# Gated cross-attention and expert layer: the waits of the first attention batch placed where they are needed, the first mask loaded early

## The chip, the cores and the metric

The kernel runs on one core of a Trainium2 chip. The metric is the device time of one execution in microseconds; the profile times every instruction and every DMA packet of one execution.

## The reference

Two layers work on 8 batches of 224 rows of 512 values. The first is a gated cross-attention: 16 heads of 32 values, 750 context rows, an integer mask. The second routes rows to 8 experts.

```python
Q, K, V = proj(_layernorm(x), W_q), proj(ctx, W_k), proj(ctx, W_v)     # Q, K turned by position
scores = jnp.einsum('bhqd,bhkd->bhqk', Q, K) / jnp.sqrt(jnp.float32(D_K))
scores = jnp.where(mask == 0, jnp.float32(-jnp.inf), scores)
attn = jax.nn.softmax(scores, axis=-1)
x = x + jnp.tanh(g_xattn[0]) * (jnp.einsum('bhqk,bhkd->bhqd', attn, V) ... @ W_o)
logits = jnp.einsum('bsd,ed->bse', _layernorm(x), gate_w)
gating, idx = jax.lax.top_k(softmax(logits).T, k)                      # k = 56 rows of 224 per expert
x = x + jnp.tanh(g_ffn[0]) * scatter(gating * (silu(x_in @ w_gate) * (x_in @ w_up)) @ w_down)
```

## The kernel before, in words

The program has three parts, one after the other; each is a block with one hand-written instruction stream per engine, and all engines meet at a barrier between blocks.

**`project_context`** (about 0 to 289 us of the span) makes K and V of all 8 batches, in four pairs. TensorE multiplies, ScalarE copies V out of PSUM (`v_out`) and makes the high half of K (`k_split`), VectorE rotates K and makes the low half. SyncE (SP), which issues most DMAs, stores both to DRAM (`k_split<-k_split`, `v_rows<-v_out`). The last pair also prepares the queries of batch 0 (`qs`). At its end GpSimd (POOL) waits for its own stores of `qs`, then loads the mask of batch 0 into `mq_first`, which lies over `q_hi`; VectorE (`mask_queries`) turns it into the float mask `mq` and only then reaches the barrier.

**`attend`** (about 301 to 870 us) runs the 8 batches. A batch has 16 turns `t`, one head each. In a turn TensorE computes the scores of the head three turns on (`m_ps<-ks,qs`, in `start()` the first three heads), VectorE adds the mask and takes the row minimum (`sm<-m_ps,mq`), ScalarE takes the exponential two turns on (`sm<-sm,least`), TensorE transposes the head in three tiles (`t_ps<-cst,sm`) into two PSUM buffers, and ScalarE or VectorE copies each to `e_t` (`DVE_TILES` says who). Four turns later TensorE multiplies by `vs` (`o_ps<-e_t,vs`). There are 8 buffers `e_t`; the first five lie where `v_out` and `k_split` of the first part were. SP loads K of two heads every second turn (`load_k`), V in two halves (`vs`), the next rows (`x_t`) and mask (`mq_raw`), and at the start `wo_sb` (1 MB) and `gw_sb`.

In `start()` of the kernel before, SP waits until all V is stored, loads `vs`, `wo_sb` and `gw_sb`, and waits until all K is stored. ScalarE waits for all stores before its first exponential, VectorE before its first copy to `e_t`, and TensorE waits for `wo_sb` and `gw_sb` (`att_in`) before its first transpose. `wo_sb` is first used at turn 5 of batch 1.

Each batch `b` also finishes batch `b - 1`. Among this is `x2_out`: two additions on VectorE, 112 x 512 each, from `x_res` to `x2o` at turn 10, which POOL then stores to `out`.

**`experts`** (870 us to the end) is bound by TensorE and is not touched.

Of the kernel before, what the change touches and what calls it, by code (L numbers as in the profile page):

```python
# [18 lines left out]
S2 = 750  # L19
# [27 lines left out]
E_OVER = HG + 1  # L47

# [24 lines left out]
class Both:  # L73
# [7 lines left out]
    mq_first: object  # L81
# [36 lines left out]
def program(nc, ctxT, x, maskq, wk, wv, wq, wo, gatew, gx, gf, wstream, consts, rotations, out):  # L118
# [5 lines left out]
    with ExitStack() as top:  # L124
# [16 lines left out]
        with ExitStack() as mid:  # L141
# [9 lines left out]
            with ExitStack() as early:  # L151
                mq_first = sb(early, "mq_first", [QP, QC, S2], I32)
# [3 lines left out]
                wraw=wraw, v_out=v_out, k_split=k_split, e_t=e_t, c_raw=c_raw, ks=ks, mq_first=mq_first, q_hi=q_hi, q_lo=q_lo,  # L156
# [19 lines left out]
def project_context(nc, sem, sb, ps, both, ctxT, wk, wv, wq, x, maskq, gx, gf, consts, rotations, kd, vd, cst, gains):  # L176

    with ExitStack() as st:
# [46 lines left out]
        with nc.Block() as block:  # L225
            @block.sync
            def _(sp):
# [54 lines left out]
                load_x(0)  # L282
                pair(0, False)
# [10 lines left out]
            def _(pool):  # L294
# [34 lines left out]
                for g in range(NG):  # L329
                    hold(qs_in[g], 48)  # L330
                pool.dma_start(both.mq_first[:], maskq[0:1].rearrange("o p c n -> p (o c) n")).then_inc(mq0_in, 16)
# [68 lines left out]
            def _(dve):  # L400
# [74 lines left out]
                def mask_queries():  # L475
                    dve.wait_ge(mq0_in, 16)
                    dve.wait_ge(fill_set, 2)
                    nc.vector.tensor_scalar(mq[:, :, 0:S2], both.mq_first[:], 0, MASKED, ALU.is_equal, ALU.mult).then_inc(mq_done, 1)

                def pair(i, last):  # L480
# [13 lines left out]
                    if last:  # L494
                        mask_queries()
# [10 lines left out]
                norm(0)  # L506
                with dve.Fori(1, B // 2 - 1) as i:
                    pair(i, False)
# [97 lines left out]
def attend(nc, sem, sb, ps, both, x, maskq, wo, gatew, kd, vd, xn_rows, out, cst, ident,  # L606
           cos, sin, gains, gate_all, row_all):

    with ExitStack() as st:
# [11 lines left out]
        e_t = both.e_t + [sb(st, f"e_t{j}", [KP, KC // 2, PAIR]) for j in range(E_OVER, 2 * HG)]  # L621
# [65 lines left out]
        with nc.Block() as block:  # L687
            @block.sync
            def _(sp):
# [32 lines left out]
                def start():  # L722
                    for k in range(KC // VT):
                        hold(v_stored[k], 16 * B)
                    load_v(0, 0)
                    sp.dma_start(wo_sb[:], wo).then_inc(att_in, 16)
                    sp.dma_start(gw_sb[:], gatew).then_inc(att_in, 16)
                    for k in range(2):
                        hold(k_stored[k], 16 * B * NG // 2)

                def body(b, j, first, last):
                    for t in range(0, H, 2):
# [11 lines left out]
                        if t == 4:  # L744
                            load_v(b, 1)
                        if t == 12 and not last:
# [9 lines left out]
            def _(pool):  # L756
# [25 lines left out]

                def spread_parts(b, q):
# [18 lines left out]
                def body(b, j, first, last):  # L802
                    for t in range(H):
# [10 lines left out]
                        if not first:  # L814
                            if t == 8:
                                root(b - 1, 1, 2 * b + 1 if last else 2 * b + 2)
                            if t == 9:
                                store_rows(b - 1)
                                store_out(b - 1)
# [6 lines left out]
                def end():  # L826
                    root(B - 1, 1, 2 * B)
                    store_rows(B - 1)
                    store_out(B - 1)
# [6 lines left out]
            def _(act):  # L836
# [45 lines left out]
                def start():  # L882
                    for k in range(KC // VT):
                        act.wait_ge(v_stored[k], 16 * B)
                    for k in range(2):
                        act.wait_ge(k_stored[k], 16 * B * NG // 2)
# [806 lines left out]
```

## Time and profile before

| | |
|---|---|
| time, median of 3 runs | 1863.48 us (1860.78 to 1865.54) |
| profiled execution: its own time | 1861.66 us |
| profiled execution: its span | 1859.8 us |
| TensorE busy | 1738.0 us (93%) |
| VectorE, ScalarE, GpSimd busy | 56%, 45%, 11% |

Times in views of the trace count from the start of the span; 1.9 us of the profiled time lie outside it. PE is TensorE, PEld its weight loads, DVE VectorE, ACT ScalarE, POOL GpSimd, SPq the queue of SyncE.

### The profile page before, as it was taken

Reading aid. Unit: us, or ns where it says so; the run is one execution under the profiler, and the core shown is the slowest. Engines: PE = TensorE matmul, PEld = TensorE weight load, DVE = VectorE, ACT = ScalarE, POOL = GpSimd, SP = SyncE. Lnnn points to the kernel's source line nnn. Section 1 sums busy time; section 2 is a strip of 40 time slices with the busy share of each in tenths; the row PEclk is TensorE's granted clock in tenths of the full one; section 3 lists DMA queues with packets and bytes.
Section 4 is the critical chain, followed back from the end, with each engine's and each line's share of the span. In section 5 each row is a group of like instructions: output and inputs, shape, how many; then the busy total and the mean of one; then the engine's idle time right before and its main releaser. Section 6 shows DMA issues by size and latency. Waiting matters only on the chain.

```text
span 1859.8 us, 28459 instructions
## 1 busy us (share of the span) xinstructions
PE 1738.0 (93%) x10502; PEld 1542.7 (83%) x10502; DVE 1044.9 (56%) x1801; ACT 840.6 (45%) x1483; POOL 204.0 (11%) x287
## 2 busy tenths in 40 slices
PE   7999993999999999993899999999999999999995
PEld 6998992778777777761899999999999999999995
DVE  6666662878877877854453544535445354353541
ACT  3232321878777777860443433434334344343430
POOL 0000010202211220201000201102001020020101
PEclk9999996999999999996899999999999999999998
DMA  6545446467567656613333533434335353353421
GB/s 235 219 177 195 175 156 186 124 141 185 139 139 178 159 134 157 158 54 103 115 107 108 142 114 112 138 105 141 113 100 152 103 141 112 102 151 104 121 101 20
DMA packets 76190, 251.90 MB, mean 135 GB/s; under 512 B 10785, under 2 KB 10785, under 8 KB 74817
## 3 DMA queue, kind: packets, MB, share of 16 engines
q1 hardware_dynamic: 63968, 215.88, 37.9%
q0 software_dynamic: 12128, 34.80, 8.1%
q8 instruction: 57, 0.93, 0.2%
q14 instruction: 37, 0.30, 0.1%
HBM read 188.01 MB, written 51.61 MB: 129 GB/s over the span
## 4 chain that ended last, share of the span: by engine, by line
PE 51%; POOL 1%; DMA 0%; DVE 0%; issue 0%; DVEq 0%; ACT 0%; POOLq 0%
PE gu_ps L1579 11%; PE gu_ps L1577 11%; PE gu_ps L1578 11%; PE y_ps L1594 6%; PE y_ps L1596 5%; PE y_ps L1595 5%; PE y_ps L1605 1%; PE gu_ps L1563 1%; DMA xg<-xn_rows,gather_i 0%; POOL out L1437 0%; POOL xg L1427 0%; DVE xs_lo L1512 0%; DVE y_cols L1539 0%; PE gu_ps L1623 0%; DVE y_sb L1517 0%
## 5 line engine op out<-in xcount | busy, mean ns | idle before, releaser
L1577 PE MATMUL gu_ps<-xs_hi,ws_hi 128*128 128x448 f32 x1024 | 371.7, 363 | 3.0 <-DVE xs_lo L1512 3.0
L1579 PE MATMUL gu_ps<-xs_hi,ws_lo 128*128 128x448 f32 x1024 | 371.8, 363 | 0.0
L1578 PE MATMUL gu_ps<-xs_lo,ws_hi 128*128 128x448 f32 x1024 | 370.5, 362 | 0.0
L1507 DVE TENSOR_TENSOR ws_lo<-w_raw,ws_hi 128x1024 fp32r<-128x1024 f32 x192 | 235.3, 1226 | 188.9 <-ACT ws_hi L1457 188.5
L1457 ACT ACTIVATE ws_hi<-w_raw 128x1024 fp32r<-128x1024 f32 x192 | 201.7, 1051 | 164.1 <-PE y_ps L1596 146.6
L1254 PEld LDWEIGHTS t_ps<-cst,sm 112*125 112x125 f32 x1536 | 204.3, 190 | 85.2 <-issue 32.4
L1254 PE MATMUL t_ps<-cst,sm 112*125 112x112 f32 x1536 | 234.0, 281 | 31.0 <-DVE e_t L978 14.3
L863 ACT ACTIVATE sm<-sm,least 112x752 f32<-112x752 f32 x256 | 234.4, 917 | 27.7 <-DMA v_rows<-v_out 16.8
L970 DVE CUSTOM_DVE_ANT_0 sm<-m_ps,mq 112x752 f32<-112x752 f32 x256 | 229.8, 935 | 29.8 <-PE m_ps L1238 28.1
L1577 PEld LDWEIGHTS gu_ps<-xs_hi,ws_hi 128*128 128x128 f32 x1024 | 192.3, 188 | 15.2 <-issue 3.3
L1578 PEld LDWEIGHTS gu_ps<-xs_lo,ws_hi 128*128 128x128 f32 x1024 | 192.3, 188 | 14.0
L1579 PEld LDWEIGHTS gu_ps<-xs_hi,ws_lo 128*128 128x128 f32 x1024 | 192.6, 188 | 12.7
L1478 ACT ACTIVATE silu<-gu_ps 128x448 f32<-128x448 f32 x128 | 69.8, 545 | 274.1 <-PE gu_ps L1579 274.1
L1594 PE MATMUL y_ps<-h_hi,ws_hi 128*128 128x448 f32 x512 | 186.2, 364 | 0.0
L1596 PE MATMUL y_ps<-h_hi,ws_lo 128*128 128x448 f32 x512 | 185.3, 362 | 0.0
L1526 DVE TENSOR_TENSOR hid<-silu,gu_ps 128x448 f32<-128x448 f32 x128 | 79.6, 622 | 188.1 <-ACT silu L1478 188.1
L1595 PE MATMUL y_ps<-h_lo,ws_hi 128*128 128x448 f32 x512 | 184.9, 361 | 0.0
L870 ACT ACTIVATE e_t<-t_ps 125x448 f32<-125x448 f32 x256 | 137.2, 542 | 104.4 <-PE t_ps L1254 102.0
L1437 POOL DMA_INDIRECT out<-y_sb,scatter_i x32 | 52.4, 1637 | 854.7 <-DVE y_sb L1517 847.4
L1238 PE MATMUL m_ps<-ks,qs 96*112 96x376 f32 x512 | 122.9, 360 | 15.7 <-PEq L225 13.5
L1529 DVE TENSOR_TENSOR h_lo<-hid,h_hi 128x448 fp32r<-128x448 f32 x128 | 80.1, 625 | 82.6 <-ACT h_hi L1480 82.6
L1480 ACT ACTIVATE h_hi<-hid 128x448 fp32r<-128x448 f32 x128 | 74.1, 579 | 88.0 <-DVE hid L1526 88.0
(146 smaller groups left out, 2408.4 us busy)
## 6 DMA issues: line engine op xcount, KB each, us to landing
w_raw<-wstream SPq DMA_DIRECT2D x192, 512.0 KB, 3.5
ks<-k_split SPq DMA_DIRECT2D x192, 188.0 KB, 5.4
k_split<-k_split SPq DMA_DIRECT2D x32, 752.0 KB, 3.4
v_rows<-v_out SPq DMA_DIRECT2D x16, 750.0 KB
vs<-v_rows SPq DMA_DIRECT2D x16, 750.0 KB
c_raw<-ctxT SPq DMA_DIRECT2D x7, 1500.0 KB, 12.8
qs<-q_hi POOLq DMA_DIRECT2D x64, 112.0 KB, 5.3
mq_raw<-maskq SPq DMA_DIRECT2D x7, 656.2 KB, 10.1
```

The source lines that it names most:

```text
L863: nc.scalar.activation(rows, rows, ACT.Exp, bias=least[:, h % KSLOTS, qc:qc + 1], scale=-1.0, accum_out=sums[:, h // HG % 2, qc, h % HG:h ...
L870: nc.scalar.activation(e_t[h % (2 * HG)][:, pc], t_ps[tile_of(b, h, pc) % 2][0:KP, 0:PAIR], ACT.Copy).then_inc(t_act, 1)
L970: nc.vector.tensor_tensor_reduce(sm[:, h % SR, qc].rearrange("p (a n) -> p a n", a=2), m_ps[qc][0:QP, :, 0:KN], mq[:, qc].rearrange("p (a ...
L1254: mm = nc.tensor.transpose(t_ps[n % 2][0:KP, a:a + QP], sm[:, h % SR, qc, c * KP:c * KP + KP], ident[0:QP, 0:QP])
L1457: nc.scalar.activation(w_hi[s][:], w_raw[s][:], ACT.Copy).then_inc(whi_done, 1)
L1507: nc.vector.tensor_tensor(w_lo[s][:], w_raw[s][:], w_hi[s][:], ALU.subtract).then_inc(wlo_done[s], 1)
L1577: nc.tensor.matmul(o, w_hi[s][:, w], xs_hi[:, c], start=(c == 0), stop=False)
L1578: nc.tensor.matmul(o, w_hi[s][:, w], xs_lo[:, c], start=False, stop=False)
L1579: mm = nc.tensor.matmul(o, w_lo[s][:, w], xs_hi[:, c], start=False, stop=(c == DC - 1))
L1594: nc.tensor.matmul(o, w_hi[s][:, w], h_hi[:, i], start=(i == 0), stop=False)
L1595: nc.tensor.matmul(o, w_hi[s][:, w], h_lo[:, i], start=False, stop=False)
L1596: mm = nc.tensor.matmul(o, w_lo[s][:, w], h_hi[:, i], start=False, stop=(i == IC - 1))
```

## The change

The mask of batch 0 is loaded by SP near the start of the program, straight into `mq`, and turned in place by VectorE after the first pair; `mq_first` goes. In `attend`, the waits for the stores move from `start()` to turn 3 of batch 0 on ScalarE and VectorE (`FREE_TILES` = 3) and to turn 8 on SP; the five `e_t` buffers over `v_out` and `k_split` are now those of heads 3 to 7. SP loads `wo_sb` and `gw_sb` at turn 6 instead of ahead of everything, and TensorE waits for them in `project_out`. `x2_out` moves from VectorE, turn 10, to GpSimd, turn 12. The diff, cut:

```diff
+FREE_TILES = 2 * HG - E_OVER
...
-            with ExitStack() as early:
-                mq_first = sb(early, "mq_first", [QP, QC, S2], I32)
...
                 load_x(0)
+                sp.dma_start(mq[:, :, 0:S2].bitcast(I32), maskq[0:1].rearrange("o p c n -> p (o c) n")).then_inc(mq0_in, 16)
                 pair(0, False)
...
-                for g in range(NG):
-                    hold(qs_in[g], 48)
-                pool.dma_start(both.mq_first[:], maskq[0:1].rearrange("o p c n -> p (o c) n")).then_inc(mq0_in, 16)
...
-                    nc.vector.tensor_scalar(mq[:, :, 0:S2], both.mq_first[:], 0, MASKED, ALU.is_equal, ALU.mult).then_inc(mq_done, 1)
+                    nc.vector.tensor_scalar(mq[:, :, 0:S2], mq[:, :, 0:S2].bitcast(I32), 0, MASKED, ALU.is_equal, ALU.mult).then_inc(mq_done, 1)
...
-                    if last:
-                        mask_queries()
...
                 moments(0)
                 norm(0)
+                mask_queries()
...
-        e_t = both.e_t + [sb(st, f"e_t{j}", [KP, KC // 2, PAIR]) for j in range(E_OVER, 2 * HG)]
+        e_t = [sb(st, f"e_t{j}", [KP, KC // 2, PAIR]) for j in range(E_OVER, 2 * HG)] + both.e_t
...
                 def start():
                     for k in range(KC // VT):
-                        hold(v_stored[k], 16 * B)
+                        hold(v_stored[k], 16)
                     load_v(0, 0)
-                    sp.dma_start(wo_sb[:], wo).then_inc(att_in, 16)
-                    sp.dma_start(gw_sb[:], gatew).then_inc(att_in, 16)
-                    for k in range(2):
-                        hold(k_stored[k], 16 * B * NG // 2)
...
+                        if t == 6 and first:
+                            sp.dma_start(wo_sb[:], wo).then_inc(att_in, 16)
+                            sp.dma_start(gw_sb[:], gatew).then_inc(att_in, 16)
+                        if t == 8 and first:
+                            for k in range(KC // VT):
+                                hold(v_stored[k], 16 * B)
+                            for k in range(2):
+                                hold(k_stored[k], 16 * B * NG // 2)
...
+                def x2_out(b, j):
+                    flag = flags_sb[:, j]
+                    hold(rest_free, R_USES * b + R_Y + 3)
+                    hold(flag_step, 5 * b + 5)
+                    hold(out_stored, 16 * b)
+                    for c in range(QC):
+                        nc.gpsimd.tensor_scalar(x2o[:, c], x2[:, c], flag[:, 3, c:c + 1], None, ALU.add).then_inc(x2o_done, 1)
...
+                            if t == 12:
+                                x2_out(b - 1, 1 - j)
                                 store_out(b - 1)
...
+                        if first and t == FREE_TILES:
+                            early_stores()
...
-                            if t == 10:
-                                x2_out(b - 1, 1 - j)
...
+                            pe.wait_ge(att_in, 32)
...
-                    pe.wait_ge(att_in, 32)
```

The order of ScalarE's instructions before, at the barrier into `attend` (`v_stored` and `k_stored` are the stores, `masked` VectorE's results):

```order
L361 ACTIVATE v_out<-v_ps1 125x2x256 [waits v_made1]
L361 ACTIVATE v_out<-v_ps2 125x2x256 [waits v_made1]
L225 UNCONDITIONAL_BRANCH
L835 UNCONDITIONAL_BRANCH [waits barrier_Pool_Activation_PE_DVE_SP_release]
L863 ACTIVATE sm,sums<-sm,least 112x752 [waits k_stored1,k_stored0,masked0,v_stored1,v_stored0]
L863 ACTIVATE sm,sums<-sm,least 112x752 [waits masked1]
```

and in the changed kernel, the last copy of turn 2 and the first rows of turn 3:

```order
L880 ACTIVATE e_t7<-t_ps0 125x448 [waits t_made]
L880 ACTIVATE e_t0<-t_ps1 125x448 [waits k_stored1,k_stored0,t_made,v_stored1,v_stored0]
L873 ACTIVATE sm,sums<-sm,least 112x752 [waits masked0]
L880 ACTIVATE e_t0<-t_ps0 125x448 [waits t_made]
L873 ACTIVATE sm,sums<-sm,least 112x752 [waits masked1]
```

The wait for the stores has moved from the first exponential to the first copy of turn 3. (Buffers carry the names they were made under: `e_t0` is now head 3's.)

GpSimd's order in batch 1, from turn 8 on, before:

```order
L774 TENSOR_SCALAR var<-mv 112x2 [waits mv_done1]
L776 TENSOR_TENSOR rstd<-var,minus_half 112x2 [waits var_done]
L796 DMA xn_rows<-xn2 112x2x512 [waits xn2_done]
L792 DMA out<-x2o 112x2x512 [waits x2o_done]
L767 DMA qs<-q_hi 32x896 [waits qlo_done,m_made]
L767 DMA qs<-q_hi 32x896
L767 DMA qs<-q_lo 32x896
L787 COPY spread<-parts 112x256 [waits parts_done,r_made]
```

and now:

```order
L803 DMA xn_rows<-xn2 112x2x512 [waits xn2_done]
L766 DMA qs<-q_hi 32x896 [waits qlo_done,m_made]
L766 DMA qs<-q_hi 32x896
L766 DMA qs<-q_lo 32x896
L794 COPY spread<-parts 112x256 [waits parts_done,r_made]
L788 TENSOR_SCALAR x2o<-x_res,flags_sb 112x512 [waits rest_free,flag_step]
L788 TENSOR_SCALAR x2o<-x_res,flags_sb 112x512
L799 DMA out<-x2o 112x2x512 [waits x2o_done]
L766 DMA qs<-q_hi 32x896 [waits qlo_done,m_made]
```

The two additions stand on GpSimd, behind the `spread` of turn 11; the store of `out` comes after them, and three loads of `qs` and the `spread` no longer stand behind it.

TensorE's order at its first transpose, before:

```order
L1238 MATMUL m_ps1<-ks,qs 112x376 [waits masked1]
L1238 MATMUL m_ps1<-ks,qs 112x376
L1254 MATMUL t_ps0<-cst,sm 125x112 [waits exp_done1,exp_done0,att_in]
L1254 MATMUL t_ps0<-cst,sm 125x112 x3
L1254 MATMUL t_ps1<-cst,sm 125x112 x4
```

and now:

```order
L1248 MATMUL m_ps1<-ks,qs 112x376 [waits masked1]
L1248 MATMUL m_ps1<-ks,qs 112x376
L1264 MATMUL t_ps0<-cst,sm 125x112 [waits exp_done1,exp_done0]
L1264 MATMUL t_ps0<-cst,sm 125x112 x3
L1264 MATMUL t_ps1<-cst,sm 125x112 x4
```

Only the wait for `att_in` has left this place.

## Rows read from the trace of the kernel before

**Rows 1.** Stretches: PE, PEld, DVE, ACT, POOL busy (count), TensorE clock, DMA share, GB/s

```profile
285.00:290.00 5.00, 2.97 (x13) 2.04 (x11) 0.94 (x1) 1.23 (x3) 0.05 (x1) 1.00 0.86 275
290.00:295.00 5.00, 0.00 (x0) 0.00 (x0) 0.00 (x0) 0.00 (x0) 0.50 (x1) 0.56 0.66 209
...
325.00:330.00 5.00, 5.00 (x32) 4.95 (x31) 4.18 (x9) 3.23 (x8) 0.00 (x0) 0.68 0.58 155
```

**Rows 2.** Who waited for whom, 280 to 330 us: total, times, longest

```profile
PE t_ps L1254 <- DMA gw_sb<-gatew: 14.2, 1, 14.2
```

**Rows 3.** Timeline around the barrier: start, us, engine, line, operation, idle before

```profile
288.67 0.29 SPq L247 DMA_DIRECT2D v_rows<-v_out  x1
300.06 0.94 DVE L478 TENSOR_SCALAR mq<-mq_first 112x1500 f32<-112x1500 int32 x1 [14.05 <-DMA mq_first<-maskq]
301.48 1.56 PE L1238 MATMUL m_ps<-ks,qs 96*112 96x376 f32 x4 [13.51 <-PEq L225]
```

**Rows 4.** Timeline of the first attention turns

```profile
302.58 0.94 DVE L970 CUSTOM_DVE_ANT_0 sm<-m_ps,mq 112x752 f32<-112x752 f32 x1 [1.15 <-PE m_ps L1238]
...
305.39 0.30 SPq L705 DMA_DIRECT2D vs<-v_rows  x1
305.40 0.92 ACT L863 ACTIVATE sm<-sm,least 112x752 f32<-112x752 f32 x1 [16.80 <-DMA v_rows<-v_out]
...
305.68 1.74 PE L1238 MATMUL m_ps<-ks,qs 96*112 96x376 f32 x4 [0.27 <-DVE least L970]
...
321.60 2.02 PE L1254 MATMUL t_ps<-cst,sm 112*125 112x112 f32 x8 [14.18 <-DMA gw_sb<-gatew]
...
330.61 0.91 PE L1238 MATMUL m_ps<-ks,qs 96*112 96x376 f32 x4
...
333.94 0.54 ACT L870 ACTIVATE e_t<-t_ps 125x448 f32<-125x448 f32 x1 [0.74 <-PE t_ps L1254]
334.11 0.91 PE L1238 MATMUL m_ps<-ks,qs 96*112 96x376 f32 x4
...
343.94 0.91 PE L1238 MATMUL m_ps<-ks,qs 96*112 96x376 f32 x4
```

**Rows 5.** TensorE's waits from 328 to 830 us

```profile
PE t_ps L1254 <- DVE e_t L978: 14.3, 23, 1.2
PE m_ps L1238 <- DVE least L970: 1.3, 7, 0.2
```

**Rows 6.** Timeline at turns 10 to 13 of batch 1

```profile
429.10 0.83 DVE L1020 TENSOR_SCALAR x2o<-x_res,flags_sb 112x512 f32<-112x512 f32 x2
...
430.61 1.10 PE L1254 MATMUL t_ps<-cst,sm 112*125 112x112 f32 x8 [0.47 <-DVE e_t L978]
...
436.10 0.94 DVE L962 TENSOR_SCALAR mq<-mq_raw 112x1500 f32<-112x1500 int32 x1
```

**Rows 7.** GpSimd's instructions from 330 to 830 us, by line

```profile
L781 POOL TENSOR_TENSOR q_rot<-q_rot,cst 128x448 f32<-128x448 f32 x14 | 16.1, 1147 | 63.8 <-DVE q_rot L1003 63.8
L787 POOL COPY spread<-parts 112x256 f32<-112x256 f32 x32 | 12.8, 401 | 273.2 <-DVE parts L985 273.2
```

**Rows 8.** Single microseconds and the start, columns as in rows 1

```profile
320.00:321.00 1.00, 0.00 (x0) 0.00 (x0) 0.00 (x0) 0.00 (x0) 0.00 (x0) 0.50 0.32 120
10.00:20.00 10.00, 7.11 (x24) 5.77 (x25) 7.19 (x11) 5.84 (x9) 0.00 (x0) 1.00 0.99 387
```

**Rows 9.** Landing of the three `ks` loads issued at 307.3 to 308.6 us

```profile
DMA to landing us min/median/max: 9.2/9.6/15.6
```

**Rows 10.** VectorE after the first pair of the first part

```profile
84.26 1.00 DVE L454 TENSOR_SCALAR xn<-x_t,mv,rstd 112x512 f32<-112x512 f32 x2 [1.33 <-POOL rstd L314]
86.01 0.01 DVE L425 LOAD_MASK_SELECT k_rot<-k_ps  x1 [0.74 <-PE k_ps L529]
```

**Rows 11.** Timeline from the last batch's `x2_out` to the barrier into `experts`

```profile
850.20 0.88 DVE L1020 TENSOR_SCALAR x2o<-x_res,flags_sb 112x512 f32<-112x512 f32 x2
...
870.84 22.51 SPq L1404 DMA_DIRECT2D w_raw<-wstream  x8
```

More of the change, by code:

```diff
@@ L80 @@
     ks: object
-    mq_first: object
     q_hi: object
@@ L150, in program @@
             ks = sb(mid, "ks", [3 * WAYS, KSLOTS, SK], F32R)
-            with ExitStack() as early:
-                mq_first = sb(early, "mq_first", [QP, QC, S2], I32)
             q_hi, q_lo = sb(mid, "q_hi", [P, NG, S], F32R), sb(mid, "q_lo", [P, NG, S], F32R)
             both = Both(
-                wraw=wraw, v_out=v_out, k_split=k_split, e_t=e_t, c_raw=c_raw, ks=ks, mq_first=mq_first, q_hi=q_hi, q_lo=q_lo,
+                wraw=wraw, v_out=v_out, k_split=k_split, e_t=e_t, c_raw=c_raw, ks=ks, q_hi=q_hi, q_lo=q_lo,
                 x_t=sb(mid, "x_t", [QP, QC, D]), xn=sb(mid, "xn", [QP, QC, D]), xT=sb(mid, "xT", [P, 2, 2 * S]),
@@ L828, in end @@
                     store_rows(B - 1)
+                    x2_out(B - 1, (B - 1) % 2)
                     store_out(B - 1)
@@ L880, in logit_exp, with early_stores @@
                     nc.scalar.activation(ex[:], lg[:], ACT.Exp).then_inc(lexp_done, 1)
-                def start():
+                def early_stores():
                     for k in range(KC // VT):
@@ L886, in start @@
                         act.wait_ge(k_stored[k], 16 * B * NG // 2)
+                def start():
                     for h in range(XLEAD):
@@ L1013, in low_q @@
                     nc.vector.tensor_tensor(q_lo[:], q_cos[:], q_hi[:], ALU.subtract).then_inc(qlo_done, 1)
-                def x2_out(b, j):
-                    flag = flags_sb[:, j]
-                    dve.wait_ge(rest_free, R_USES * b + R_Y + 3)
-                    after(dve, out_stored, 16 * b)
-                    for c in range(QC):
-                        nc.vector.tensor_scalar(x2o[:, c], x2[:, c], flag[:, 3, c:c + 1], None, ALU.add).then_inc(x2o_done, 1)
                 def flags(b, j):
                     flag = flags_sb[:, j]
+                    after(dve, x2o_done, QC * (b - 1))
                     for qc in range(QC):
@@ L1084, in start, with early_stores @@
                             mask_scores(0, h, qc)
+                def early_stores():
                     for k in range(KC // VT):
@@ L1107, in body @@
                                 normalise(b - 1, t // HG + 2)
+                        if first and t == FREE_TILES:
+                            early_stores()
                         for pc in range(KC // 2):
@@ L1159, in end @@
                     norm_2(b)
-                    x2_out(b, b % 2)
                     logits(b)
```

## The prediction

> **What bounds the kernel now.** I read the busy time by stretch first, then the waits of the stretch that stood out, then its timeline. TensorE is busy 93% of the span; the gap that this change can touch lies between the first part and the attention, from 289 to 330 us. There the engines stand still and TensorE's granted clock falls: the stretch from 290 to 295 us shows no matmul and a clock of 0.56, that from 325 to 330 us a full engine at 0.68 [rows 1]. So a full stop and a restart at the lower of the two levels (1.2 instead of 2.4 GHz) lie one behind the other.
>
> The stop has two halves. In the first, SP's last issue ends at 288.96 us, but VectorE sits until 300.06 us for the mask, works 0.94 us on it, and TensorE starts 0.48 us after that, at 301.48 us [rows 3]. In the second, TensorE has its first three heads' scores at 307.4 us (305.68 + 1.74) and starts its first transpose at 321.60 us [rows 4]; the waits name the load of `gw_sb` [rows 2], 16 KB that stand behind `vs` and 1 MB of `wo_sb` in SP's queue. ScalarE's own wait, for the last V store, ended at 305.40 us [rows 4], so it was not the last to end. Later, the attention is close to TensorE's pace: from 328 to 830 us it waits 15.6 us for VectorE in all [rows 5].
>
> **The change part by part.**
>
> *The mask.* Its load and VectorE's work leave the barrier. The last to reach it is then SP at 288.96 us; with the same 0.48 us TensorE starts at 289.44 us. That is 12.0 us earlier. What it needs there is old: `ks` and `qs` of the first heads have landed. The new place costs a load of 656 KB behind those of the start: at 387 GB/s [rows 8] 1.7 us of all DMA engines. I take 0, since what TensorE starts on is queued ahead of it and the stretch after it is not full; the other bound is 1.7 us. VectorE's 0.94 us go behind the work that ends at 85.26 us, where it idles 0.74 us before the next one at 86.01 us [rows 10]: 0.2 us is late, and the next waits of VectorE there are longer. 0, at most 0.2 us.
>
> *The wait for `wo_sb` and `gw_sb`.* After the first scores, nothing but the exponentials of head 0 stands ahead of the first transpose. From 301.48 to 307.42 us the scores took 5.94 us, paced by VectorE's masks; so they end at 295.4 us (289.44 + 5.94), and the exponentials of head 0 (the first mask 1.10 us after TensorE's start [rows 4], two masks and two exponentials of 0.9 us each) by 294.2 us. The first transpose goes from 321.60 to 295.4 us: 26.2 us, which includes the 12.0. The wait itself, now in `project_out` of batch 1, comes a whole batch after the load (14 turns of 3.5 us or more): 0. If the cover were gone it would cost the load's own time there.
>
> *The waits for the stores.* They now stop ScalarE and VectorE at turn 3. ScalarE's first copy of turn 3 was at 333.94 us, 12.3 us after the first transpose, so it comes at about 306 (307.7 at the old clock, 305.4 with the next term). The last V store, issued at 288.67 us, was seen by ScalarE at 305.40 us [rows 3, 4], and then shared the engines with the mask load, which is gone. I take 0 us; the far bound is a store that is slowed by the loads that now follow, see the second rival. The copies of turns 0 to 2 go into memory that no store reads.
>
> *The clock.* From the first transpose to the scores of head 5 took 9.01 us (321.60 to 330.61), mostly at the lower level; one turn at the full level takes 3.50 (330.61 to 334.11) [rows 4]. The stretch is two turns and half a microsecond, 7.5 us. TensorE now stops only from 288.0 (2.97 us of work after 285) to 289.4 us and then works in short pieces; before, it stood idle from 288.0 and the clock was still full for most of a microsecond after 290 us [rows 1]. I take it as staying full: 1.5 us, and 0.4 us in the first scores. Bounds: 0 and 1.9 us.
>
> *`x2_out`.* VectorE had 0.83 us of it at 429.10 us; its next copy ended late and TensorE waited 0.47 us [rows 6], and a little later 0.19 us for a mask, seven times in all [rows 5]. The pair recurs in each of batches 1 to 7. Removing it is worth 0.47 x 7 = 3.3 us; bounds 0 (another wait takes its place) and 0.66 x 7 = 4.6 us. In the last batch it lies 20 us ahead of the barrier at 870.8 us [rows 11] beside TensorE's own work: 0. On GpSimd the trace has no such operation. Its copy takes 1.57 ns a column (401 for 256), its product of two tensors 2.56 (1147 for 448) [rows 7]; so 0.8 to 1.3 us for each of the two, 1.6 to 2.6 us a batch. Behind it in GpSimd's queue are the store of `out`, three loads of `qs` for the next batch's head 12, and the next `spread`, four turns (14 us) after the one ahead of it. 0.
>
> The sum against the profiled execution: 1861.66 - 26.2 - 1.9 - 3.3 = 1830.3 us. The median of the runs shown is 1.8 us above that execution, so 1832.0 us.
>
> One rule speaks against moving `x2_out`. In rows, VectorE's mask of 1500 columns takes 0.94 us at 436.10 us [rows 6], 7 us after the old place of `x2_out`; the additions on GpSimd wait for the `spread` that follows VectorE's work just ahead of 429.1, so they should lie between 430 and 433. The Trainium skill (SBUF — State Buffer, Who interferes with whom) says that GpSimd shares a port pair with VectorE, that VectorE's two-port modes and its operations with two SBUF inputs meet it there, and that the later one blocks for the other's whole length. By the rule the sum stays if they don't overlap, and becomes the third rival if they do.
>
> **The rivals.**
>
> *The clock falls in the first scores.* For it: pieces of TensorE's work there wait on VectorE. Against: no gap is as long as that before the fall. Then the 1.9 us are not gained: 1833.9 us.
>
> *The loads come late.* SP's queue seems served in order on the engines that a transfer uses: `gw_sb`, 16 KB, landed only at 321.6 us, after all that was ahead [rows 2]. V's transfers keep a third of the engines: at 320 us the share is 0.32 [rows 8]. The first `vs` was issued at 305.39 us and the `ks` of head 8, behind it, landed 15.6 us after the last of them was issued at 308.6 us [rows 9], at 324.3: 18.9 us, of which `wo_sb` (1 MB over all engines, at 387 or 209 GB/s [rows 1, 8]) is 2.7 to 5.0. Now `vs` stands behind the V store, which ends at 305.4 us, or up to 2 us earlier without the mask load beside it; `ks` lands, without `wo_sb`, at 317 to 321 us if the rest is as slow as before, or at about 312 if `vs` (750 KB at 120 GB/s [rows 8], 6.4 us) and 3 us for `x_t` and `ks` are all. Head 8's scores were at 343.94 us [rows 4], now 28.1 us earlier, at 315.8. I take 313 to 314 and no stall, since fewer loads compete; else 1 to 5 us are lost: about 1835 us. The Trainium skill (DMA: Bandwidth & Descriptors, Why a DMA increments its semaphore by 16 and not by 1) says that a copy runs on the largest number of engines up to 16 that divides its outer dimension: 5 for 125 partitions. The share of 0.32 agrees, and the rule makes this rival's queue a real one.
>
> *GpSimd and VectorE meet.* If `x2_out` on GpSimd holds up a VectorE operation by its own length, 1.3 us a batch, the 0.47 us are not gained and 0.4 to 1.3 us is lost, 7 times: 1838 to 1844 us.
>
> *Slower than before.* The same addition on GpSimd, but so slow that its queue is what TensorE waits for: `spread` of turn 15 is due some 12 us after `x2_out` starts, with 2 us of issues between. Up to 10 us for the pair nothing is lost; each further microsecond costs 7. From 14.5 us a pair the kernel is slower than before, and at 16 us it takes 1832 + 7 x 6 = 1874 us. That is six times the bound from the product's row: unlikely.
>
> *It doesn't do what it says.* Another wait of `start()` keeps the attention where it was, the V store above all: then the exponentials start at 305.4 us as before and the first transpose 1.8 us later, at 307.2 instead of 295.4: 1844 us. Against: the first three copies lie in free memory.
>
> **How the numbers follow.** My forecast has 0.62, the clock 0.12, late loads 0.12, GpSimd against VectorE 0.06, the store in another place 0.04, slower 0.02, and 0.02 for no change. The range from 1827 to 1839 us takes in the whole bound of `x2_out` and the medians' spread below (1.3 + 1.9 and a little), and the clock, the late loads and the lower end of the third rival above. The forecast's own range is 1828 to 1835. Within 0.3%, 5.6 us, is about what a measurement can tell from no change; all cases but the last two are faster by more: 0.96, 0.02, 0.02.
>
> **What would show it.** Right: the first scores 12 us earlier; the first transpose near 295 us and not behind a load; no wait at ScalarE's first copy of turn 3; the clock at 1.00 through the change of parts; each batch from the second on 0.5 us shorter, with TensorE's 0.47 us wait gone at turn 12; the last part the same length. Wrong: a wait for `ks`, `vs` or a store in turns 3 to 9, VectorE operations stretched beside GpSimd's additions, or a longer first pair.

## The result, and the profile after

| | before | after |
|---|---|---|
| median of the timed executions | 1863.55 us (4) | 1840.47 us (4, 1838.09 to 1842.64) |
| the profiled execution: time, span | 1861.66, 1859.8 us | 1842.64, 1840.8 us |
| TensorE busy, mean clock | 93%, 0.974 | 94%, 0.978 |

The ratio is 0.9876, with a 95% interval of 0.9864 to 0.9888: 23 us faster. The forecast of 1832.0 us is 8.5 us too low, and the measured median lies 1.5 us above the upper end of the range. The changed kernel's four times fall in two pairs, 1838.1 and 1838.5, 1842.5 and 1842.6 us, and the trace below is of the slowest. One execution of the kernel before, timed beside the first four experiments, took 3526.8 us and stands in none of the ratios.

The row that names the start of the change of parts, from the timeline of the changed kernel:

```profile
289.32 0.29 SPq L245 DMA_DIRECT2D v_rows<-v_out  x1
290.53 0.07 DVE L1089 MEMSET flags_sb<- 112x16 f32 x1 [3.87 <-PEq L223]
290.55 2.92 SPq L700 DMA_DIRECT2D vs<-v_rows  x1
290.64 0.57 PE L1248 MATMUL m_ps<-ks,qs 96*112 96x376 f32 x2 [2.03 <-PEq L223]
...
296.02 1.86 PE L1264 MATMUL t_ps<-cst,sm 112*125 112x112 f32 x8
```

Against [rows 3, 4] the first scores come 10.8 us earlier (301.48 to 290.64) and the first transpose 25.6 us earlier (321.60 to 296.02), with no wait for a load. The waits for a store are gone from this place, and none appears at turn 3.

The stretches after it (us, busy time of PE, PEld, DVE, ACT, POOL, granted clock, DMA share, GB/s):

```profile
290.00:295.00 5.00, 3.34 (x10) 1.78 (x10) 3.50 (x8) 2.64 (x5) 0.00 (x0) 0.78 0.42 145
295.00:300.00 5.00, 4.88 (x23) 4.71 (x23) 3.35 (x9) 3.14 (x8) 0.00 (x0) 0.54 0.73 250
300.00:305.00 5.00, 4.54 (x35) 3.99 (x34) 4.82 (x11) 4.57 (x10) 0.00 (x0) 1.00 0.88 234
...
340.00:345.00 5.00, 0.49 (x4) 0.31 (x3) 1.29 (x4) 1.78 (x4) 0.40 (x1) 0.90 0.64 170
345.00:350.00 5.00, 5.00 (x20) 4.88 (x21) 2.94 (x7) 2.49 (x5) 0.00 (x0) 0.50 0.33 112
350.00:355.00 5.00, 5.00 (x34) 3.75 (x34) 3.92 (x8) 2.36 (x7) 1.47 (x3) 0.58 0.84 185
```

The clock, which was to stay full, drops to the lower of its levels (1.2 instead of 2.4 GHz) twice: at about 293 us, and again at 344 us, behind a stretch in which TensorE is busy for 0.49 of 5 us. The timeline says what that stretch is:

```profile
312.51 5.63 SPq L695 DMA_DIRECT2D ks<-k_split  x3
...
336.96 0.92 PE L1248 MATMUL m_ps<-ks,qs 96*112 96x376 f32 x4
...
344.77 1.59 PE L1248 MATMUL m_ps<-ks,qs 96*112 96x376 f32 x4 [4.51 <-DMA ks<-k_split]
345.91 0.94 DVE L984 CUSTOM_DVE_ANT_0 sm<-m_ps,mq 112x752 f32<-112x752 f32 x1 [4.62 <-PE m_ps L1248]
```

These are the scores of heads 13 and 14 of batch 0. Those of head 14 wait 4.5 us for a load of `ks`, and then take 1.59 us instead of 0.92 for the clock. Its three issues go from 312.51 to 318.1 us. The last one, at 317.36, landed 27.4 us later, at 344.8 (view of the tile, these three issues):

```profile
L695 SPq DMA_DIRECT2D ks<-k_split x3: 428/772/4341, 312.5 to 317.4; - x3
...
DMA to landing us min/median/max: 4.8/8.2/27.4
```

TensorE's waits from 305 to 830 us, the answer to [rows 5]:

```profile
PE t_ps L1264 <- DVE e_t L992: 11.1, 16, 1.2
PE o_ps L1288 <- issue: 5.0, 8, 0.9
PE m_ps L1248 <- DMA ks<-k_split: 4.5, 1, 4.5
PE t_ps L1264 <- ACT e_t L880: 3.5, 16, 0.4
```

And `x2_out` on GpSimd, 330 to 830 us:

```profile
L788 POOL TENSOR_SCALAR x2o<-x_res,flags_sb 112x512 f32<-112x512 f32 x14 | 21.9, 1570 | 0.0
```

Where the forecast gain went is read from the starts of the scores, head by head (heads of batch 1 counted on from 16), and from the first `w_raw` load, 850.43 us now:

| place | before | after | earlier by | forecast |
|---|---|---|---|---|
| first scores | 301.48 | 290.64 | 10.8 | 12.0 |
| head 5 | 330.61 | 304.39 | 26.2 | 28.1 |
| head 8 | 343.94 | 318.45 | 25.5 | 28.1 |
| head 13 | 362.49 | 336.96 | 25.5 | 28.1 |
| head 14 | 365.56 | 344.77 | 20.8 | 28.1 |
| head 16 | 372.25 | 354.47 | 17.8 | 28.1 |
| first `w_raw` | 870.84 | 850.43 | 20.4 | 31.4 |
| end of the span | 1859.8 | 1840.8 | 19.0 | 31.4 |

So 12.4 us are missing in this pair of executions: 1.9 by head 5, 0.7 at head 8, 7.7 from head 13 to 16, 0.7 in `x2_out`, and 1.4 in the last part, whose waits of TensorE are the same in both traces. The length of that part varied from 988.0 to 990.5 us over all traces of this study, so 1.4 us is within its scatter. The 7.7 us were to be explained first.

### The profile page after: what moved, and what is told of

The parts are those of the page before. It is cut to its first block, busy times and chain, and to the rows that moved or that the text cites. A ratio compares the mean times of both kernels' runs of the same rounds, so it can differ in the third digit from the quotient of the medians.

```text
span 1840.8 us, 28481 instructions
## 1 busy us (share of the span) xinstructions
PE 1739.0 (94%) x10502; PEld 1547.1 (84%) x10502; DVE 1039.0 (56%) x1785; ACT 840.3 (46%) x1483; POOL 233.5 (13%) x302
## 4 chain that ended last, share of the span: by engine, by line
PE 52%; POOL 1%; DMA 0%; DVE 0%; issue 0%; DVEq 0%; ACT 0%; POOLq 0%
PE gu_ps L1588 11%; PE gu_ps L1586 11%; PE gu_ps L1587 11%; PE y_ps L1603 6%; PE y_ps L1605 6%; PE y_ps L1604 6%; PE y_ps L1614 1%; PE gu_ps L1572 1%; DMA xg<-xn_rows,gather_i 0%; POOL out L1446 0%; POOL xg L1436 0%; DVE xs_lo L1521 0%; DVE y_cols L1548 0%; PE gu_ps L1632 0%; DVE y_sb L1526 0%
```

## Experiments

Each set of runs was timed beside its own executions of the kernel before, whose median moved between 1862.7 and 1865.1 us. Across sets the ratios therefore compare better than the medians.

The theory: V's stores and loads (125 partitions) run on five of the 16 DMA engines (a share of 0.31; [rows 8] has 0.32), everything that is issued behind them has a share on these five, and moving the attention 26 us forward without moving the queue brings TensorE to a load of `ks` that isn't there.

### Which load stands in the way (a1, a2, a3, e2)

```diff
# a1, a3: turn 14; e2: turn 2
-                        if t == 6 and first:
+                        if t == 14 and first:
                             sp.dma_start(wo_sb[:], wo).then_inc(att_in, 16)
# a2, a3
-                        if t == 4:
+                        if t == (8 if first else 4):
                             load_v(b, 1)
```

> The changed kernel with the loads of wo_sb and gw_sb issued at turn 14 of batch 0 instead of turn 6. Theory 1 (a queue on the engines that V's transfers use, in which everything issued early in batch 0 stands in line): wo_sb and gw_sb are issued at 311.4 to 311.9 us, between ks of head 12 (landed 333.7) and ks of head 14 (landed 344.7), and gw_sb landed at 341.3. Without them ks of head 14 lands at 336 to 340 us, TensorE's 4.5 us wait at head 14 shrinks to under 1 us or goes, and the second fall of the clock at 344 us with it: 4 to 7.7 us faster, 1833 to 1837 us. Rival (the queue is made by V's transfers alone, wo_sb spread over all engines costs it next to nothing): ks of head 14 still lands at 343 to 345 us and the time stays within 1 us of 1840.5.

> The changed kernel with the load of the second half of V of batch 0 (vs, 750 KB on five engines) issued at turn 8 instead of turn 4; wo_sb stays at turn 6. Theory 1 (the five engines are the queue): it stood ahead of ks of heads 12 and 14, so these land about 6 to 9 us earlier (12: 333.7 to about 326; 14: 344.7 to about 336), the stall at head 14 and the second fall of the clock go: 5 to 7.7 us faster, 1833 to 1835.5 us. The half itself is needed at turn 13, and lands by about 345, in time or 1 to 2 us late. Rival (wo_sb is the load that makes ks late): under 2 us faster.

> The changed kernel with both moved: the second half of V to turn 8 and wo_sb, gw_sb to turn 14. Theory 1: no wait of TensorE for ks at head 14, clock 1.00 from 300 us on: 1832.5 to 1834.5 us, 6 to 8 us faster. If the stall was not what made the clock fall at 344 us: only 4 to 5 us faster.

> The changed kernel with wo_sb, gw_sb issued at turn 2 of batch 0 instead of 6, ahead of ks of heads 10 to 14. Theory (one queue, served in order: what stands ahead of ks is what makes it late, and for ks of head 14 the sum ahead of it is the same): head 14 waits as in the changed kernel, and ks of head 10 and 12 land 3 us or more later than there (323.2 and 333.7), in time still: 1839 to 1843 us. Rival (an early wo_sb is spread over idle engines and out of the way): 1834 to 1836 us, as a1.

| | median us | ratio to before, 95% interval |
|---|---|---|
| a1, `wo_sb` at turn 14 | 1834.24 | 0.9850 (0.9827 to 0.9874) |
| a2, second half of V at turn 8 | 1839.83 | 0.9874 (0.9851 to 0.9897) |
| a3, both | 1834.25 | 0.9841 (0.9824 to 0.9859) |
| e2, `wo_sb` at turn 2 | 1838.12 | 0.9860 (0.9844 to 0.9877) |

a1 is what the theory said. The stall is gone from TensorE's waits, the stretches behind it show no fall (the first fall, at the change of parts, is still there), and head 16 starts at 344.59 us, 27.7 us earlier than before the change. The stretches in a1:

```profile
340.00:345.00 5.00, 4.27 (x41) 3.62 (x41) 5.00 (x14) 4.18 (x11) 1.48 (x3) 1.00 1.00 209
345.00:350.00 5.00, 5.00 (x55) 4.04 (x58) 4.72 (x9) 4.79 (x11) 0.00 (x0) 1.00 1.03 204
350.00:355.00 5.00, 4.64 (x39) 3.84 (x32) 4.06 (x12) 4.39 (x10) 0.40 (x1) 1.00 1.04 204
```

Its last `ks` load of head 14 was issued at 311.84 us and landed at 329.9, 8 us before the scores at 337.90 and 6 us earlier than the theory had it. Of the 14.9 us by which it lands earlier than in the changed kernel, 5.5 are its earlier issue (311.84 for 317.36). The view of that tile:

```profile
DMA to landing us min/median/max: 18.1/18.1/18.1
```

By the medians a1 gains 6.2 us on the changed kernel, by the ratios 4.8 us, and the two intervals just overlap; d1 against d3 below, which differ in the same edit and were timed in one set, do not.

The median of a3 lies where the theory had it, and is no better than that of a1. Its trace has no stall at head 14, but the clock, which was expected to be full from 300 us on, is not. It falls once more, between heads 11 and 12, where no load is late:

```profile
330.00:335.00 5.00, 3.50 (x29) 2.09 (x30) 3.38 (x7) 3.48 (x9) 3.25 (x7) 0.86 0.82 224
335.00:340.00 5.00, 5.00 (x40) 4.39 (x40) 1.81 (x4) 3.77 (x9) 1.28 (x3) 0.80 0.67 173
```

The section on c1 to c4 comes back to this.

a2 missed its forecast by 4 us or more. Its time is the one that the rival gave (under 2 us faster), but its trace shows another reason. `ks` of head 14 was early enough, but that of head 8, which nothing in the edit touches, landed 22.0 us after 298.84, at 320.9. TensorE waited for it and the clock fell there, and once more at 335 to 340 us; from the timeline and the stretches of a2:

```profile
320.98 1.56 PE L1248 MATMUL m_ps<-ks,qs 96*112 96x376 f32 x4 [2.21 <-issue]
```

```profile
320.00:325.00 5.00, 4.02 (x24) 3.47 (x28) 3.76 (x9) 1.56 (x5) 0.94 (x2) 0.58 0.34 106
```

The wait is put down to "issue"; its end and the landing agree. In the changed kernel the same load landed at 318.4 (297.88 + 20.5), in a1 at 315.2 (295.70 + 19.5): head 8 is on the edge, and in these traces it holds TensorE up by 0 to 2.5 us. e2 shows the same. Its `wo_sb` went ahead of the loads of heads 10 to 14, the stall at head 14 was gone, and one at head 8 (2.4 us) had come, so my reading of the queue as strictly in order was too simple: what is issued behind a load can slow it too. Nor do bytes alone explain it: 1 MB over 16 engines is 64 KB on each, less than half of the 150 KB that a load of V puts on each of five, and yet in a1 the last load for head 14 landed 14.9 us earlier without it. How `wo_sb` delays these loads so much is not shown. At 1838.12 us e2 ended 2 us ahead of the changed kernel, a little better than expected, and 4 behind a1; its interval overlaps that of the changed kernel.

### Five engines or something else (a4)

```diff
-                    sp.dma_start(vs[a][:].rearrange("p c n -> p (c n)"),
-                                 vd[ds(b, 1), a].rearrange("o p n -> p (o n)")).then_inc(vs_in[a], 16)
+                    for rows in (slice(0, 112), slice(112, KP)):
+                        sp.dma_start(vs[a][rows].rearrange("p c n -> p (c n)"),
+                                     vd[ds(b, 1), a, rows].rearrange("o p n -> p (o n)")).then_inc(vs_in[a], 16)
```

and the same for the stores of `v_out`, with counts of 32 for 16 where they are waited for.

> The changed kernel with each store and load of V written as two, 112 and 13 partitions instead of 125, everything else the same. Theory 1 (125 partitions go by five engines, 150 KB on each of a 750 KB load; 112 and 13 go by 16 and 13): packets of vs and v_rows show on 16 engines, vs of batch 0 lands in half the time, ks of heads 8 to 14 each land several us earlier, no stall at head 14, no second fall of the clock: 1832 to 1835 us, if the added issues (0.3 us each, 48 of them on SP) cost nothing. Rival (the engines are held up by something else, as the number and size of the rows in each transfer): the packets take as long as before and ks of head 14 is as late, 1840 us or more.

Measured: 1836.64 us, ratio 0.9860 (0.9838 to 0.9881), an interval that overlaps that of the changed kernel; the reading rests on the traces. The microsecond from 292 us, with V's store and the load behind it under way, first in the changed kernel, then in a4, and behind it the view of the last two `ks` issues of head 8 in a4:

```profile
292.00:293.00 1.00, 0.62 (x2) 0.27 (x2) 1.00 (x3) 0.64 (x1) 0.00 (x0) 0.88 0.30 121
```

```profile
292.00:293.00 1.00, 0.73 (x4) 0.74 (x4) 0.07 (x1) 0.00 (x0) 0.00 (x0) 0.83 0.98 239
```

```profile
L696 SPq DMA_DIRECT2D ks<-k_split x2: 419/420/420, 296.3 to 296.8; - x2
DMA to landing us min/median/max: 6.5/7.6/8.8
```

The share goes from 0.30 to 0.98, and the last `ks` load of head 8 lands 8.8 us after 296.79, at 305.6 us instead of 318.4. Nothing but the way in which V's transfers are cut was changed, so that is the cause; that it is five engines and no other number is read from the share alone. Neither the stall at head 14 nor the second fall is in this trace. The time is 1.6 us above the upper end of what was expected, and the price is in SP's row: the last two stores hold the barrier, and the first scores start at 292.26 us, 1.6 us later than in the changed kernel.

### The parts one by one (b1 to b4, e1)

b1 is the kernel before with the mask lines of the diff alone, b4 with `x2_out` alone. b2 and b3 are the changed kernel with the mask, and with `x2_out`, put back. e1 is b2 with `wo_sb` at turn 14.

> The kernel before with the mask part of the change alone (loaded early into its place, worked on behind the first pair); the waits of start() and x2_out as before. Theory A (the two halves of the stop are not a sum: the wait for gw_sb hangs on SP's queue, which starts with the last V store and not with the barrier): first scores at about 290.5 us, 11 us earlier, but the first transpose only 0 to 3 us earlier, at 318 to 322 us, so 0 to 4 us faster: 1860 to 1863.5 us. Theory B (the two parts add, as the 12.0 us in the prediction's first step read): 11 to 12 us faster, 1851.5 to 1852.5 us.

> The changed kernel with the mask as before (loaded by GpSimd behind the copies of q, worked on ahead of the barrier): so the moved waits and x2_out alone. Theory A: the barrier stays at 301 us and the first transpose comes straight behind the first scores, at about 307 us instead of 321.6: 14.5 us, with 2.3 us for x2_out 16.8 us faster than before, 1846.7 us; the queue of loads starts at about 302 us, a little ahead of where it would be, so head 14 waits for its ks no longer than in the changed kernel, and the clock falls as there: up to 4 us are lost again, 1847 to 1851 us. Theory B (what b1 gives is what is missing here): 1850 to 1852 us.

> The changed kernel with x2_out back on VectorE at turn 10 of the next batch. Theory by the traces (a batch went from 65.63 to 65.30 us): 0.33 us a batch is given back, 7 times: 2.3 us slower, 1842.8 us. By the prediction's size (0.47 us a batch): 3.3 us slower, 1843.8 us. Rival (x2_out was worth nothing, the batch's period differs by something else of the change): within 0.5 us of 1840.5.

> The kernel before with x2_out on GpSimd alone. Theory by the traces: each batch from the second on 65.30 instead of 65.63 us, 2.3 us faster than before: 1861.2 us. By the prediction's size 3.3 us, 1860.2 us. Rival as in b3: within 0.5 us of 1863.5.

> The kernel of b2 (mask as before, waits and x2_out as changed) with wo_sb, gw_sb at turn 14. Theory (b2 had no load that came late and no second fall, so there is nothing for this edit to give): within 1 us of b2, 1843 to 1845 us. With a1 it then tells what the mask part alone is worth once the loads keep up: about 9.5 us, against 3.3 us in the changed kernel. Rival (moving wo_sb is worth 6 us by itself, wherever the attention starts): 1837 to 1838 us.

| | median us | ratio to before, 95% interval |
|---|---|---|
| b1, mask alone | 1859.27 | 0.9984 (0.9974 to 0.9994) |
| b2, waits and `x2_out` | 1843.74 | 0.9897 (0.9881 to 0.9913) |
| b3, changed kernel, `x2_out` back | 1842.74 | 0.9880 (0.9861 to 0.9898) |
| b4, `x2_out` alone | 1859.65 | 0.9985 (0.9975 to 0.9995) |
| e1, b2 with `wo_sb` at turn 14 | 1845.04 | 0.9901 (0.9884 to 0.9917) |

*Mask and waits.* Alone the mask is worth 3 us (1 - 0.9984 of 1863; 1 to 5 by the interval), as theory A of b1 had it: the first scores came at 289.99 us and TensorE then stood for the load of `gw_sb`:

```profile
PE t_ps L1248 <- DMA gw_sb<-gatew: 22.4, 1, 22.4
```

The waits alone brought more than either theory of b2 allowed. Its trace has no wait for a load and no second fall, and head 16 starts at 354.73 us, where it does in the changed kernel (354.47), although that one had begun the attention 8.5 us earlier (290.64 against 299.19). So most of the mask part was eaten: it is worth 3.3 us in the changed kernel (1843.74 to 1840.47; 3.9 by the ratios). With `wo_sb` late it is worth 10.8 us (e1, 1845.04, to a1, 1834.24; 9.5 by the ratios), and late `wo_sb` gives e1 nothing over b2. So what makes `wo_sb` costly is the attention that starts early. I read it so that the stop at the barrier had been the time in which V's last store drained: in b2 that store was issued at 288.47 us and the first load of `vs` only at 299.10, and from 295 to 300 us the share is 0.32. No view gives the store's own landing.

*`x2_out`.* A batch takes 65.63 us before, 65.30 after, 65.30 in b4 and 65.66 in b3 (distance of the first scores from batch to batch): 0.33 us a batch, whatever else stands. The times agree, with 2.3 us in b3 and 2.8 in b4. b4's interval excludes that it is worth nothing; b3's is too wide to tell it from the changed kernel.

### The clock without a stall (c1 to c4)

```diff
# c1, c4: behind each half of the first scores
+                            if h or qc:
+                                fill(3 if h == 0 else 1)
# fill(n): n times
+                        nc.tensor.matmul(w_ps[0:QP, 0:2 * S], qs[:, 0, 0:QP], qs[:, 0:2, :], start=True, stop=True)
```

c2 is a1 with V's loads split as in a4, c3 is a4 with `wo_sb` as in a1, c4 is c2 with the added matmuls.

> The changed kernel with added matmuls on TensorE (448 columns of qs into w_ps, read by nobody) in the gaps of the first scores: three behind head 0, one behind each later half. It adds 7 matmuls of about 0.27 us and takes nothing away. Theory (the clock falls at 291 to 300 us because TensorE stops at the barrier and then works in short pieces, and this costs about 1 us in the first scores and 1 us behind): with the gaps filled the clock stays higher or comes back earlier, the first transpose comes 0 to 0.5 us earlier and head 5 up to 1.5 us earlier, 0 to 2 us faster, unless the stall at head 14 takes it back. Rival (the stop of 2 us at the barrier itself is enough): the clock falls as before, the time is within 0.5 us of 1840.5, or up to 0.5 us slower by the fillers.

> The kernel of a1 (wo_sb, gw_sb at turn 14) with only the loads of V, and not its stores, written as 112 and 13 partitions. Theory: in a1 no wait of TensorE for a load was left, so the faster landing is worth nothing there: within 1 us of a1, 1834.2 us. Rival (loads that land earlier free something else): 1832 to 1833 us.

> The kernel of a4 (stores and loads of V split) with wo_sb, gw_sb at turn 14 as in a1. Theory: a4 had neither the stall nor the second fall, so what moving wo_sb adds is nothing; the last store has two issues on SP, the barrier comes 0.3 to 2 us later than in a1: 1835 to 1837 us. Rival (the two edits add): 1830 to 1832 us.

> The kernel of c2 with the added matmuls of c1. By the theory of c1, 0 to 2 us faster than c2: 1832 to 1834 us, and here no stall can take it back; by its rival, as c2.

Measured: c1 1841.41 us (0.9879, interval 0.9864 to 0.9894), c2 1836.96 (0.9845, 0.9831 to 0.9858), c3 1836.30 (0.9851, 0.9837 to 0.9864), c4 1835.14 (0.9838, 0.9825 to 0.9852). c2's median lies 2.7 us from a1's where 1 was allowed, but by the ratios (0.9845, 0.9850) the two are alike. c4 is 1.1 us above its range. The added matmuls give nothing that can be told. The clock in c1, where TensorE is busy throughout:

```profile
290.00:295.00 5.00, 5.00 (x17) 3.73 (x16) 4.37 (x9) 3.67 (x7) 0.00 (x0) 0.56 0.35 129
```

So the gaps between the first scores don't bring it down. What is left is the stop of 1.7 us at the barrier or something ahead of it, as c1's rival had it; its time is 0.4 us above that rival's range. Which of the two it is was not tested.

c2's trace held something else. No load is late, and yet its clock fell at about 332 us:

```profile
325.00:330.00 5.00, 3.33 (x20) 2.19 (x18) 4.86 (x13) 3.60 (x8) 0.40 (x1) 1.00 0.07 23
330.00:335.00 5.00, 4.23 (x31) 3.00 (x32) 2.18 (x5) 2.32 (x8) 4.45 (x9) 0.68 0.92 243
335.00:340.00 5.00, 5.00 (x35) 4.07 (x35) 1.81 (x4) 3.61 (x8) 0.08 (x1) 0.64 0.29 84
```

These are turns 7 to 9 of batch 0, where VectorE is busy for 4.86 of 5 us and TensorE waits 0.9 and 1.2 us for its copies. a1 has the same gaps at 323.8 and 327.6 us and the clock stays at 1.00. Without a disturbance, heads 8 to 16 take 28.3 us (a1, a4, b1, b2, c4); in c2 they take 31.3, in a3 29.8 and in c3 29.6, so this fall costs 1.3 to 3 us in the traces that have it. In a2, c1 and e2 it comes on top of a late load. That makes 6 of the 16 traces without the edit that follows. The Trainium skill (TensorE: Matmul & The Clock Gate, What's actually happening) says that the window over which the gate watches activity runs freely, not in step with the kernel. Two executions with the same gaps that come out differently agree with it.

### Holding the clock there (d1 to d4)

```diff
                         next_scores(1)
+                        if first and t in (7, 8):
+                            fill_rows(4 if t == 7 else 6)
# fill_rows(n): a wait until w_ps is free, then n times
+                        nc.tensor.transpose(w_ps[0:QP, 0:QP], ident[0:QP, 0:QP], ident[0:QP, 0:QP])
```

> The kernel of a1 (wo_sb, gw_sb at turn 14) with added transposes on TensorE (112 columns of ident into w_ps, read by nobody): four behind the scores of turn 7 and six behind those of turn 8 of batch 0, where TensorE waits 0.9 and 1.2 us for VectorE's copies. Theory (there is a second place where the clock can fall in batch 0, these thin turns, apart from the stall for ks: in c2 and c3 it fell at 331 us without any stall, in a1 and c4 with the same waits it did not): with the gaps filled it doesn't fall there in any execution; heads 8 to 16 take 28.3 us, the median comes down from 1834.2 to 1832 to 1834 and its spread narrows. Rival (the fall in c2 came from something else, as the barrier's): it can still fall, and the time is that of a1.

> The kernel of d1 with the added matmuls in the first scores as well. By the clock theory 0 to 1 us faster than d1: 1831 to 1833.5 us. By the rival as d1.

> The changed kernel (wo_sb, gw_sb at turn 6 as in it) with the added transposes of d1 alone. Theory (in the changed kernel it is the 4.5 us stall at head 14 for ks that costs, and the fall behind it): the added work does nothing for it, head 14 waits as before, 1839 to 1841.5 us. Rival (the thin turns are what costs, and the stall is hidden slack): 1834 to 1836 us.

> All together: wo_sb, gw_sb at turn 14, V's loads as 112 and 13 partitions, added work in the first scores and in turns 7 and 8. If the split loads are worth nothing where no load is late, as d2: 1831 to 1833.5 us. The rest that this leaves against the prediction's 1832.0 us is the clock's first fall (up to 1.9) and x2_out's smaller share (1.0).

| | median us (lowest to highest) | ratio to before, 95% interval |
|---|---|---|
| d1, a1 with work in turns 7 and 8 | 1833.41 (1832.45 to 1835.84) | 0.9848 (0.9834 to 0.9861) |
| d2, and in the first scores | 1832.97 (1832.42 to 1837.27) | 0.9845 (0.9831 to 0.9858) |
| d3, changed kernel with work in turns 7 and 8 | 1840.64 (1840.35 to 1841.29) | 0.9882 (0.9867 to 0.9897) |
| d4, d2 with V's loads split | 1832.39 (1831.12 to 1832.85) | 0.9840 (0.9826 to 0.9853) |

d3 settles the main question: with the thin turns filled the changed kernel is as slow as ever, and its trace has the stall at head 14 and the fall behind it:

```profile
PE m_ps L1248 <- DMA ks<-k_split: 4.1, 1, 4.1
```

d1, with `wo_sb` late and the same fills, was timed in the same set: 1833.41 us against 1840.64, and the two intervals are apart. So the late load is what costs, and the thin turns don't explain it.

Whether the fills help once the stall is gone is not shown. None of d1 to d4 has the fall at turns 7 to 9, but 10 of the 16 traces without fills have none either, and d1 against a1 is 0.8 us, inside the intervals. The spread within d2 has its cause in its trace, `ks` of head 8 at 319.6 us and TensorE 2.5 us late for it. In d4, with V's loads split, that load lands at 312.4 us (296.26 + 16.1), and its five times lie within 1.8 us. It has the lowest median of all, 8 us below the changed kernel (6.7 by the ratios), but c4 (0.9838), a3, d2 and d1 cannot be told from it. It contains matmuls whose results nobody reads.

## Why the prediction was wrong

*The mask, and the wait for `wo_sb` and `gw_sb`: right, slightly over.* First scores 10.8 us earlier for 12.0, first transpose 25.6 for 26.2. The handover from SP's last issue to the first scores took 1.03 us for 0.48 (0.68 in a1, b1 and b3), and SP's last issue came 0.65 us later than before. I don't put that on the early load: with it the first copy of V lies between 22.4 and 23.4 us in the changed kernel, a1, a2, b1 and b3, and without it at 22.30, 22.09 and 22.98 us (before, b2, b4).

*The stores at turn 3: right, 0.* 

*The clock: wrong, and the first rival in kind.* The term was 1.9 us for "staying full", and the clock fell at 293 us. At head 5 also 1.9 us are missing, but that the numbers agree is chance: 1.2 of them are the late start. From the first scores to head 5 the forecast had 13.07 us (289.44 to 302.51), the trace has 13.75, and without any gain it would have been 14.97. So the term gave 1.2 us of its 1.9. c1 shows that the gaps in the first scores, the reason that was weighed, don't decide it.

*The loads: this is the step that failed.* The second rival was named with 0.12, placed at head 8 and priced at 1 to 5 us, and the forecast took "313 to 314 and no stall, since fewer loads compete". It landed at 318.4 us, inside the slower case of my own bracket (317 to 321), and cost 0.7 us. The larger part lay where I had not looked: only head 8 was followed, though `wo_sb`, `gw_sb` and the second half of V, moved or kept behind it, stand ahead of `ks` of head 14. I asked for the first load behind the slow ones instead of for each up to the last, and the signs named cover turns 3 to 9, while the stall came in turn 11. And the price left out what a stall of 4.5 us does to the clock: 7.7 us in all from head 13 to 16, where the sum had 0. With `wo_sb` moved out of the way (a1, d1) the medians are 1834.2 and 1833.4 us, inside the forecast's own range. Nor did the sum ask what the removed stop had been good for: V's store drained in it, as b2 against the changed kernel suggests.

*`x2_out`: right in kind, over in size.* 2.6 us in the trace for 3.3. TensorE's wait of 0.47 us at turn 12 is gone, and 0.33 us a batch is what is left of it, since new small waits stand in its place: 8 for `o_ps` with 5.0 us in all, against 3 with 1.6 before; b4 has 9 with 5.5. On GpSimd each addition takes 1.57 us, above the bound of 1.3 us, and no wait of TensorE is put down to it. No operation of VectorE was stretched beside it in batch 1, the one that I read: the pair lies from 411.93 to 415.07 us, and the scores' masks beside it, at 412.61 and 414.30 us, take 0.94 and 0.93 us, as those at 410.28 and 415.16 us do. The mask of 1500 columns, which the prediction feared for, comes only at 417.57 us. So the third rival did not come, and what an overlap with that mask would cost was not seen.

*Slower, and "it doesn't do what it says": no.*

What stays open: which of the four timed executions of the changed kernel have the stall, and how long, since only the slowest has a trace; why 1 MB of `wo_sb` delays the loads of `ks` as much as it does; whether the stop at the barrier or something ahead of it brings the clock down; and whether a handover of 1.03 or 0.68 us is more than chance.

## What to carry to other kernels

When a wait goes, ask what ran in its shadow. Here it was, as I read it, a store on five engines. Then follow every load that the earlier stage needs, up to the last one that was issued behind the slow transfer, and not only the first. Here a stall of 4.1 to 4.5 us on TensorE cost 2.5 to 3.2 us more for the clock (the changed kernel, b3, d3), and one of 2.2 us (c1, head 14) was followed by no fall. With the transfers over 125 partitions written as 112 and 13, the load of head 8 behind them landed in less than half the time (8.8 for 20.5 us); and a load that is needed a batch later belongs behind the last one that is needed now.

## What the runs showed of the hardware

- Of the three `ks` loads of a pair of heads, which count on one semaphore, two are seen to land within 4 to 9 us and the third after 20 to 27 (heads 8 to 14 of the changed kernel; 4.8/8.2/27.4 above); with V split, in a4, none of them takes over 10 us. The Trainium skill (DMA: Bandwidth & Descriptors, Why a DMA increments its semaphore by 16 and not by 1) says that each engine posts its own share of a copy's 16, and that copies in flight on one semaphore fill each other's counts. If each of the three loads runs on all 16 engines, eleven free ones times three is 33, two full counts. That fits, and was not tested.
- SP's own issues take longer in this queue. The row at 290.55 us shows 2.92 us for one issue of `vs`, where the store at 289.32 us took 0.29; the first of the three issues of `ks` for head 14 took 4.3 us, and the other two come behind it.
- GpSimd took 1570 ns to add a column to 112x512, VectorE 0.83 us for two of these [rows 6]: nearly four times as long.
